# Near products on halves of the rows in the attention of an adaLN layer

## What is computed

```python
scores = jnp.einsum('bhid,bhjd->bhij', q, k)
rel = jnp.einsum('bhid,pd->bhip', q, rel_key)                 # p = 512
rel_idx = jnp.clip(j - i + p - 1, 0, p - 1)
bias = jnp.take_along_axis(rel, rel_idx, axis=3)              # constant for j <= i - 511
logits = jnp.where(j <= i, (scores + bias) * scale, -jnp.inf)
attn = jax.nn.softmax(logits, axis=-1)
```

## Time and profile before

| | us |
|---|---|
| median of three runs | 3829.51 |
| the profiled execution | 3828.18 |
| its span, first to last instruction | 3826.1 |
| TensorE (PE) busy | 3288.1 (86%) |
| VectorE (DVE) busy | 2352.2 (61%) |
| ScalarE (ACT) busy | 1461.1 (38%) |
| GpSimd (POOL) busy | 1393.6 (36%) |

### The profile page before, as it was taken

One profiled execution on the slowest core, in us unless ns is written; L12 is line 12 of the kernel. 1 busy time (PEld: TensorE's weight loads), 2 busy tenths in 40 slices (PEclk: granted clock), 3 DMA queues, 4 the chain that ended last, 5 costly groups with the idle time before them and its releaser, 6 DMA issues. The chain is left out here.

```text
span 3826.1 us, 173211 instructions
## 1 busy us (share of the span) xinstructions
PE 3288.1 (86%) x76960; PEld 2814.2 (74%) x76960; DVE 2352.2 (61%) x4756; ACT 1461.1 (38%) x1765; POOL 1393.6 (36%) x1575
## 2 busy tenths in 40 slices
PE   6876999889999999898999998989999889389980
PEld 5456888777888877787888777878888777368770
DVE  6855666665365776644667666446676662365774
ACT  3631333344422333353223333532333346245551
POOL 5754332322353332225533322345332211212556
PEclk8988999998998999899999898999999999689995
DMA  5952110000311100003111000131110000444654
GB/s 142 246 163 76 35 33 21 28 21 25 107 48 37 38 30 17 29 16 120 43 30 38 30 26 20 39 100 43 39 31 17 25 13 12 143 139 150 193 174 132
DMA packets 243388, 255.20 MB, mean 67 GB/s; under 512 B 99496, under 2 KB 186380, under 8 KB 242524
## 3 DMA queue, kind: packets, MB, share of 16 engines
q1 hardware_dynamic: 222204, 202.68, 17.6%
q0 software_dynamic: 20448, 41.45, 3.6%
HBM read 151.36 MB, written 92.59 MB: 64 GB/s over the span
## 5 line engine op out<-in xcount | busy, mean ns | idle before, releaser
L959 DVE TENSOR_TENSOR att_acc<-att_pm,att_acc 128x512 f16<-128x512 f32 x1920 | 1248.1, 686 | 615.8 <-PE att_pm L1066 330.8
L1039 ACT ACTIVATE att_pt<-att_ps 128x1024 f32<-128x1024 f32 x560 | 573.9, 1025 | 1448.8 <-PE att_ps L1069 1446.8
L1066 PE MATMUL att_ps<-att_qx,table_x 68*128 68x64 f16 x8960 | 727.6, 194 | 4.9 <-issue 4.9
L1069 PE MATMUL att_ps<-att_qz,table_z 128*128 128x64 f16 x8960 | 724.8, 194 | 3.1 <-issue 3.0
L1042 ACT ACTIVATE att_pt<-att_ps 128x1024 f32<-128x1024 f32 x528 | 513.0, 1024 | 468.9 <-PE att_ps L1079 456.3
L1166 PE MATMUL att_po<-att_pt,att_vn 128*32 128x128 f32 x17408 | 634.5, 289 | 4.4 <-issue 4.0
L149 POOL TENSOR_TENSOR att_qx<-att_qe,mask_i 64x1024 f16<-64x1024 f16 x128 | 239.5, 1888 | 1056.4 <-PE att_po L1166 1013.9
L1069 PEld LDWEIGHTS att_ps<-att_qz,table_z 128*128 128x128 f16 x8960 | 618.5, 99 | 5.0 <-issue 4.9
L1066 PEld LDWEIGHTS att_ps<-att_qx,table_x 68*128 68x128 f16 x8960 | 615.6, 99 | 5.9 <-issue 5.7
L1166 PEld LDWEIGHTS att_po<-att_pt,att_vn 128*32 128x32 f32 x17408 | 471.6, 115 | 64.9 <-issue 19.1
L1062 PE MATMUL att_ps<-att_qs,att_kn 113*128 113x64 f16 x8960 | 454.1, 194 | 39.0 <-DMA att_qs<-s_m 37.1
(11 more groups left out here) (211 smaller groups left out, 4055.7 us busy)
## 6 DMA issues: line engine op xcount, KB each, us to landing
att_qe<-s_q SPq DMA_DIRECT2D x256, 128.0 KB
moe_xs<-s_h SPq DMA_DIRECT2D x78, 256.0 KB
s_y<-moe_y SPq DMA_DIRECT2D x78, 256.0 KB, 2.4
s_v<-att_vn SPq DMA_DIRECT2D x32, 512.0 KB, 5.3
att_vn<-s_v SPq DMA_DIRECT2D x64, 256.0 KB, 3.1
att_qs<-s_q SPq DMA_DIRECT2D x128, 66.0 KB
att_kn<-s_k SPq DMA_DIRECT2D x128, 64.0 KB, 2.4
att_x<-in_x SPq DMA_DIRECT2D x64, 128.0 KB
```

The costliest lines, as they stand in the source:

```text
L959: dve.tensor_tensor(held, got, held, ALU.max).then_inc(bank_done, 1)
L1039: act.activation(pt[:, k % 2, :, t * 64:t * 64 + 64].rearrange("p h (x c) -> p x h c", x=2), ps[t][:, :, :].rearrange("p x (h c) -> p x h ...
L1066: last = pe.matmul(groups[:, :, g], keep["table_x"][:, y:y + P], qx[0:G * D + G, s, x * (XQ // G) + g], start=False, stop=(g == XQ // G - ...
L1069: last = pe.matmul(groups[:, :, g], keep["table_z"][:, y:y + P], qz[:, s, x * (XQ // G) + g], start=False, stop=(g == XQ // G - 1), skip_g ...
```

## The change

A near pair is now worked on in halves t of 64 queries (XQ = 64), and heads 0 to 7 and 8 to 15 each have a half of the partitions and a bank of their own. `qs` holds the queries once, without the zeros. The table lies in both halves of the partitions, high and low part as two slices (`keep["table"]`), and the low products are matmuls of their own: three products a group in the exact pass, one in the maxima, each as a pair of 8 x 4 = 32 columns, one for each half. In the exact pass the causal mask is one product of `later` and `equal` with 512 columns for each bank of a diagonal block; in the maxima pass it is a minimum with `bound`, in the first (diagonal) step's VectorE instruction. The maxima's row takes part in the exact pass alone. `bank` waits for two free banks ahead of near pairs too. `expand_groups` runs twice a block on 128 partitions. The planner's costs are set anew.

```diff
 def expand_groups(...):
-    s, u = n % SLOTS, quarter % 2
-    rows, dst = (G * D, att.qx) if quarter < 2 else (P, att.qz)
+    return pool.tensor_tensor(att.qx[:, n % SLOTS, part],
+                              att.qe[:, n % 2, part].rearrange("p h (g i) -> p g h i", i=G),
+                              keep["mask_i"][:, :].unsqueeze(1).unsqueeze(1).broadcast_to([P, NG, HH, G]), ALU.mult)
...
-                    for dst, row, part in (("table_x", 0, 0), ("table_z", 0, 1), ("table_z", G, 0)):
-                        sp.dma_start(keep[dst][(row + i) * D:(row + i + 1) * D, :], io["s_rel"][part][:, seen]).then_inc(table_in, 16)
+                    for part in range(2):
+                        for u in range(2):
+                            sp.dma_start(keep["table"][(u * G + i) * D:(u * G + i + 1) * D, part], io["s_rel"][part][:, seen]).then_inc(table_in, 16)
...
-    XQ = P // 4
+    XQ = P // 2
...
-    place_time = lambda i, j, part: 1.0 if part == 2 else 1.5 if near(i, j) else 0.45
-    step_time = {"near": 0.46, "far": 0.22, ...
+    place_time = lambda i, j, part: 1.0 if part == 2 else 1.0 if near(i, j) else 0.25
+    step_time = {"near": 0.25, "far": 0.13, ...
...
-                            dve.tensor_scalar(held, got, LOWEST, None, ALU.max).then_inc(bank_done, 1)
+                            dve.scalar_tensor_tensor(out=held, in0=got, scalar=LOWEST,
+                                                     in1=keep["bound"][:, r // 2, :].unsqueeze(1).broadcast_to([P, HH, XQ]),
+                                                     op0=ALU.max, op1=ALU.min).then_inc(bank_done, 1)
...
-                def near_scores(bank, keys, n, j, x, exact):
-                    s, rows = n % SLOTS, 64 + KM + 1
-                    pairs, groups = ...
+                def near_scores(banks, keys, n, j, t, exact):
+                    s, last, diagonal = n % SLOTS, [None, None], exact and n % NB == j
+                    groups = [b.rearrange("p (h g i) -> p h g i", h=HH, i=G) for b in banks]
                     for h in range(HH):
-                        pe.matmul(pairs[:, :, h], keys[0:rows, h, :], qs[0:rows, s, :, h, x * XQ:(x + 1) * XQ],
-                                  start=(h == 0), stop=False, skip_group_check=True)
+                        for e in range(2):
+                            rows = slice(64 * e, 64 * e + KM + exact)
+                            pe.matmul(banks[e][:, h * XQ:(h + 1) * XQ], keys[rows, h, :], qs[rows, s, h, t * XQ:(t + 1) * XQ],
+                                      start=(h == 0), stop=False, skip_group_check=True)
+                    if diagonal:
+                        for e in range(2):
+                            rows = slice(64 * e, 64 * e + 64)
+                            pe.matmul(banks[e], keep["later"][rows, t], keep["equal"][rows].rearrange("p h c -> p (h c)"),
+                                      start=False, stop=False, skip_group_check=True)
+                    products = ((0, 0), (1, 0), (0, 1)) if exact else ((0, 0),)
                     for g in range(XQ // G):
...
-                        last = pe.matmul(groups[:, :, g], keep["table_x"][:, y:y + P], qx[0:G * D + G, s, x * (XQ // G) + g],
-                        if exact:
-                            last = pe.matmul(groups[:, :, g], keep["table_z"][:, y:y + P], qz[:, s, x * (XQ // G) + g],
+                        for table, part in products:
+                            for e in range(2):
+                                rows = slice(64 * e, 64 * e + 64)
+                                last[e] = pe.matmul(groups[e][:, :, g], keep["table"][rows, table, y:y + P],
+                                                    qx[rows, s, part, t * (XQ // G) + g], start=False, stop=...
...
-                    if kind == "far" and r % 2:
+                    pair = kind in ("near", "far")
+                    if pair and r % 2:
                         return
-                    bank_free(pe, number)
+                    bank_free(pe, number + pair)
```

More of the change, by code:

```diff
@@ L222, in _ @@
                 pool.memset(keep["ident_h"][:, :], 0.0)
-                pool.memset(after[:, :], -MASK)
+                pool.memset(keep["later"][:, :, :], -1.0)
+                pool.memset(keep["equal"][:, :, :], MASK)
+                pool.memset(keep["bound"][:, :, :], -LOWEST)
                 pool.memset(keep["mask_i"][:, :], 1.0)
@@ L243, in _ @@
                 last.then_inc(pool_step, 1)
[L244 to L249, removed]
                 pool.memset(att.kn[:, :, :, :], -1.0)
-                pool.wait_ge(pool_step, 8)
+                pool.wait_ge(pool_step, 12)
             @block.scalar
@@ L647, in phase_attention @@
     TAIL = 4
-    place_time = lambda i, j, part: 1.0 if part == 2 else 1.5 if near(i, j) else 0.45
-    step_time = {"near": 0.46, "far": 0.22, "turn": 0.44, "rows": 0.12, "norm": 0.44, "back": 0.22, "out": 0.43,
+    place_time = lambda i, j, part: 1.0 if part == 2 else 1.0 if near(i, j) else 0.25
+    step_time = {"near": 0.25, "far": 0.13, "turn": 0.44, "rows": 0.12, "norm": 0.44, "back": 0.22, "out": 0.43,
                  "turn_h": 0.22, "logit": 0.9, "count": 0.3}
@@ L665, in phase_attention @@
         end = 0.4 if late else 1.0
-        line = [((at - (s[3] % 2 if s[0] == "far" else 0) + 0.5) / len(maxima) * end, 0, at, s) for at, s in enumerate(maxima)]
+        line = [((at - s[3] % 2 + 0.5) / len(maxima) * end, 0, at, s) for at, s in enumerate(maxima)]
         line += [((at + 0.7) / 5.5 * 0.45, 1, at, s) for at, s in enumerate(turning)]
@@ L832, in expand @@
                     pool.wait_ge(qe_in[n % 2], n // 2 * 64 + 64)
-                    for quarter in range(4):
-                        last = expand_groups(pool, keep, first, n, quarter)
+                    for part in range(2):
+                        last = expand_groups(pool, keep, first, n, part)
                     last.then_inc(spread, 1)
@@ new lines, in near_scores @@
+                    if diagonal:
[4 more added lines that the diff above has]
+                    products = ((0, 0), (1, 0), (0, 1)) if exact else ((0, 0),)
+                    for g in range(XQ // G):
+                        y = REL0 + 1 - G - (n % NB - j) * P - (t * XQ + G * g)
+                        for table, part in products:
+                            for e in range(2):
+                                rows = slice(64 * e, 64 * e + 64)
+                                last[e] = pe.matmul(groups[e][:, :, g], keep["table"][rows, table, y:y + P],
+                                                    qx[rows, s, part, t * (XQ // G) + g], start=False,
+                                                    stop=(g == XQ // G - 1 and table == 0 and part == exact), skip_group_check=True)
@@ L1071, in near_scores, with far_scores @@
                     return last
-                def far_scores(banks, n, j, t):
+                def far_scores(banks, n, j, t, exact):
                     s, last = n % SLOTS, [None, None]
@@ L1077, in far_scores @@
                         for e in range(2):
-                            rows, head = slice(64 * e, 64 * e + KM + 1), HH // 2 * t + h
-                            last[e] = pe.matmul(banks[e][:, h * P:(h + 1) * P], kn[rows, j, head, :], qs[rows, s, e, head, :],
+                            rows, head = slice(64 * e, 64 * e + KM + exact), HH // 2 * t + h
+                            last[e] = pe.matmul(banks[e][:, h * P:(h + 1) * P], kn[rows, j, head, :], qs[rows, s, head, :],
                                                 start=True, stop=True, skip_group_check=True)
@@ L1085, in bank @@
                     b, i = divmod(n, NB)
-                    if kind == "far" and r % 2:
+                    pair = kind in ("near", "far")
+                    if pair and r % 2:
                         return
-                    bank_free(pe, number)
+                    bank_free(pe, number + pair)
+                    if pair:
+                        banks = [full[:, :], pm[(number + 1) % NBUF][:, :]]
                     if kind == "near":
@@ L1097, in bank @@
                             pe.wait_ge(kv_in[j], b * 80 + 80)
-                        last = near_scores(full[:, :], kx[:, j] if early else kn[:, j], n, j, r, False)
+                        first_half, last = near_scores(banks, kx[:, j] if early else kn[:, j], n, j, r // 2, 0)
+                        first_half.then_inc(bank_full, 1)
                     if kind == "far":
-                        bank_free(pe, number + 1)
-                        first, last = far_scores([full, pm[(number + 1) % NBUF]], n, j, r // 2)
-                        first.then_inc(bank_full, 1)
+                        first_half, last = far_scores(banks, n, j, r // 2, 0)
+                        first_half.then_inc(bank_full, 1)
                     if kind == "turn":
```

83 lines of the change are left out of this document (34 added, 49 removed).

## The result

| | before | after |
|---|---|---|
| median of the runs, us | 3829.95 | 4682.44 |
| span of the profiled execution, us | 3826.1 | 4680.6 |
| TensorE busy, us | 3288.1 | 3544.5 |
| matmuls | 76,960 | 122,016 |
| mean granted clock | 0.924 | 0.787 |

A forecast was written before the change was run, and what follows sets the result against it. The prediction took TensorE, busy for 91% of the attention phase, as the bound; 3828 - 521 (near pairs) + 28 (mask) + 20 (change-overs) + 125 (banks) = 3480, with some 20 for the clock 3500 us, range 3420 to 3880.

The forecast's parts named there:

- the price X: Near pairs' 32-column products: a pair of halves costs 16 ns, so 280 near pairs give 521 us back.
- the first rival: Near-pair matmuls have a least time, X between 22 and 29 ns: middle 3755 us; 28 in 100.
- The upper bound: Near-pair products: X at most 31 ns, from 7.7 ns an instruction; that end takes 17 us.
- The right mechanism: Near pairs' instructions don't arrive fast enough: 3933 us at 31 ns a pair of halves; 17 in 100.
- nothing faster than the 14 ns of today: Near pairs: a pair of halves costs 56 ns, +1154 us, near 5000 us; 5 in 100.
- Bank term: Near maxima: waiting for two free banks adds 125 us, bounds +40 and +250.
- The mask product: 64 diagonal blocks: two more pairs of 512 columns each, 28 us added.
- the maximum with a bound: VectorE's maximum gets a second, broadcast input, 256 times: 686 ns against 684, so 0 us.
- change-overs: TensorE switching between half-array and whole-array work: +20 us, bounds -40 and +80.
- idle put down to issue inside the products: Table products: TensorE idle for issue there would show the forecast wrong; no size given.
- the queue's share of 1.7%: Instruction queue: a share well over 1.7%, from 1.1%, would show the forecast wrong.
- The clock: TensorE's granted clock falls where it idles for VectorE; more such idling costs some 20 us.

The follow-up runs named there:

- e2: The changed kernel with 64 columns in each table product in place of 32, same number of instructions: 4677.46 us, ratio 1.2145.
- e10: The changed kernel with the two exact products that share their weights issued as one of 64 columns, 35,840 instructions fewer: 4163.57 us.
- e3: The changed kernel without the two low table products in the exact pass, 71,680 instructions fewer: 3710.73 us.
- e11: The changed kernel with a fourth product, low table by low queries, in the exact pass, 35,840 instructions more: 5207.13 us.
- e1: The changed kernel with each near group issued as all matmuls of heads 0 to 7, then all of heads 8 to 15: 5421.74 us.
- e6: The kernel before with each near table product's weight load issued twice, 26,880 loads more: 4572.08 us.

## Why the prediction was wrong

**The step that failed** is the price X of a pair of halves with 32 columns: 16 ns were taken, with 31 ns as the highest bound, where the supply of instructions sets some 56 ns (four instructions at 14 ns). Both bounds were made wrongly. The lower one, 16 ns by the line through 64 and 128 columns, does not hold: in 1128.55 a pair takes 25 ns at full clock. This much was the first rival, and the figure of the Trainium skill ("TensorE: Matmul & The Clock Gate", section "Wait - 56ns, not 53.3ns?", no start to start under about 25 ns) is just what the trace shows, for each half. By itself it would still have left a gain: 0.93 + 128 x 0.025 = 4.13 us a near pair for 4.84.

The upper bound was the real mistake. 7.7 ns an instruction came from seven instructions behind one released wait. That is far less than a page, and inside a page the changed kernel runs at 6.2 ns an instruction (25 ns for the four of a pair): the row showed how fast instructions in hand are started, not how fast new ones come. The rate over a long stretch stood in the prediction too, 14 to 16 ns, and was taken as what TensorE happened to ask for. It was also nearly what can be had: a near pair of before, 320 instructions in 4.84 us, takes 15.1 ns for each, 3.9 us a page. The change asked for 640, 2.5 pages, at least 2.5 x 3.5 = 8.8 us. With 280 such pairs that is 1100 us more by the lowest price of a page; 852 were measured. What makes up the 250 us between them stays open. Before, TensorE idled for 263 of the 2900 us, mostly for other engines, and a page that comes during such a wait costs nothing; that this is the difference is argued, not shown.

**The rivals.** The right mechanism was there with 17 in 100, and of these 5 for "nothing faster than the 14 ns of today", near 5000 us: right in kind, 320 us too high. The reason given against it was that burst. The packet's own time (1.09 us) was taken as the supply's price "if they came without a break". It is not: in none of the twelve runs does an instruction packet start less than 3.2 us after the one before, though TensorE waits for them.

**Bank term.** The wait for two banks is +123 us in the kernel before, alone, where +103 and +125 were worked out: right in mechanism and size. In the changed kernel the near maxima's idle time rose from 37.3 to 121.6 us, 63 of them ended by VectorE, though VectorE itself idles for 1009.6 us before its maxima. What this is worth beside the page stalls was not measured there: no run takes the second bank's wait out of the changed kernel.

**The mask product** takes, at full clock, the 0.22 us of the forecast for two matmuls of 512 columns side by side (1151.57 to 1151.79):

```profile
1151.57 0.39 PE L1057 MATMUL att_ps<-equal,later 64*128 64x512 f16 x2
1151.79 0.93 PE L1065 MATMUL att_ps<-att_qx,table 64*128 64x32 f16 x62
```

**The rest**: the maximum with a bound is 685 ns (684 before), VectorE's busy time is unchanged, GpSimd's fell by 245 us and it waits for TensorE all the more (1802.0 us), and the planner's costs moved less than 1%. The 20 us for change-overs were not taken alone by any run. Halves do run side by side, as read from L1079. Of what was named as a sign that the forecast is wrong, "idle put down to issue inside the products" and pairs 25 ns apart were the ones to be seen; the queue's share of 1.7% was not reached (1.4%), because the span grew along with the 966 packets.

**The clock** fell to 0.77 in the attention, far more than was behind the 20 us allowed for it. Here it costs nothing that can be measured: e2 has 0.94 there and the same time, with more columns.

## What to carry to other kernels

Count the instructions of TensorE, weight loads included, and set them against the time: where a stretch would come under some 14 ns each (3.5 us a page of 256), as this one did, a split into more and smaller matmuls is paid by the instruction, not by the column. A burst behind a wait is no rate; take the rate from a stretch longer than a page. When columns are free, as in e2, the way to gain is fewer and wider matmuls, as in e10, which is 519 us faster than the changed kernel, though still 8% slower than the kernel before.

## What the runs showed of the hardware

Instructions of TensorE come in packets of 16.4 KB, 256 instructions. When it outruns them, it stops from page to page, with 256 instructions from restart to restart, and a page costs 3.5 to 3.8 us: e3, e10, e11. A packet itself takes 1.1 us (1.4% of 16 engines' 4680 us over 966). The packets come one at a time: TensorE restarts some 2.4 us after a packet's start, and the next packet starts 1.1 to 1.6 us after that restart (after and e2 at the places shown), never less than 3.2 us after the one before. Why the next one is not sent for earlier, and whether another load on the memory would change the price, no run here shows. That stays open.

From start to start on one half of the rows, a matmul of 32 columns takes 25 ns at the full clock (after, 1128.55) and 27 at the lower level (e1, 1122.65). So at 32 columns the lower level costs almost nothing, while eight matmuls of 64 columns take 0.42 us in place of 0.23.

More busy time did not go with a higher granted clock here: it was 0.63 in e1's attention, with TensorE busy for 97% of it, and 0.94 in e2's:

```profile
300.00:4030.00 3730.00, 2776.78 (x114041) 2341.47 (x114040) 1790.90 (x3542) 1048.87 (x1061) 748.05 (x1045) 0.94 0.11 31
```

There TensorE is busy for 74%. What the clock follows was not tested.

A second weight load ahead of one matmul is not hidden: 27 ns for each (e6).
